# Conv layer on one core: the statistics matmuls issued one product earlier, the warm-up matmuls moved, the bias added to two images in one call

## The reference

```python
x = x + conv(group_norm(x, G=16), weight, bias)      # x: (8, 32, 128, 128) float32, weight (32, 32, 3, 3)
```

## Time and profile before

| | |
|---|---|
| median of 9 runs | 86.98 us (86.24 to 87.39) |
| the profiled execution | 86.84 us |
| its span in the profile | 85.5 us |
| busy in the span | PE 68.8, DVE 50.1, ACT 48.0, POOL 32.2 us |
| bytes moved | 33.63 MB, mean 393 GB/s over the span |

### The profile page before, as it was taken

The page is one execution under the profiler, slowest core; times in us unless marked ns, Lnnn a source line. Parts: engine busy times, 40 slices in busy tenths (PEclk is TensorE's granted clock), DMA queues, the critical chain, the costliest instruction groups (busy, mean ns, idle before and its releaser), DMA issues.

```text
span 85.5 us, 726 instructions
## 1 busy us (share of the span) xinstructions
PE 68.8 (80%) x238; PEld 42.8 (50%) x238; DVE 50.1 (59%) x43; ACT 48.0 (56%) x55; POOL 32.2 (38%) x52
## 2 busy tenths in 40 slices
PE   0011996999899989998999899989989998999300
PEld 0011453567466646674666466456746664667100
DVE  0028905971998299649946992899199815200510
ACT  6008915995796299439935992699179726000000
POOL 6729400039294005904900680076009401920000
PEclk9999999999999999999999999999999999999998
DMA  3899999999999979997998995988989488999966
GB/s 50 318 401 425 414 467 406 437 421 437 421 490 490 429 306 490 490 460 306 460 429 383 414 490 245 490 352 383 490 368 421 192 368 368 471 383 405 427 260 265
DMA packets 2209, 33.63 MB, mean 393 GB/s; under 512 B 256, under 2 KB 288, under 8 KB 416
## 3 DMA queue, kind: packets, MB, share of 16 engines
q1 hardware_dynamic: 2208, 33.62, 93.6%
HBM read 16.84 MB, written 16.78 MB: 393 GB/s over the span
## 4 chain that ended last, share of the span: by engine, by line
PE 59%; ACT 17%; DMA 8%; DVE 8%; issue 2%; SPq 1%
PE ps L380 50%; ACT g L346 12%; DMA x<-x_dram 8%; PE ps_w L413 4%; PE ps_m L308 3%; ACT std L326 3%; ACT square L315 3%; DVE rstd L332 2%; DVE var L320 2%; DVE x L395 2%; DVE rstd L329 2%; PE ps_w L253 1%; SPq L175 1%; ACT origin L283 1%
## 5 line engine op out<-in xcount | busy, mean ns | idle before, releaser
L380 PE MATMUL ps<-g,w_sb 128*128 128x363 f32 (+1 forms) x192 | 61.0, 466 | 3.1 <-ACT origin L283 2.2
L380 PEld LDWEIGHTS ps<-g,w_sb 128*128 128x128 f32 x192 | 35.1, 189 | 24.3 <-ACT origin L283 5.8
L275 DVE TENSOR_REDUCE sums<-x 128x1 f32<-128x4096 f32 (+1 forms) x9 | 35.4, 3937 | 6.2 <-DMA x<-x_dram 6.2
L364 POOL TENSOR_SCALAR x<-x,bias_sb 128x1984 f32<-128x1984 f32 (+1 forms) x16 | 24.3, 1528 | 23.1 <-ACT origin L283 18.1
L294 ACT ACTIVATE unused<-x,origin 128x4096 f32<-128x4096 f32 (+1 forms) x9 | 30.0, 3329 | 0.3
L395 DVE SCALAR_TENSOR_TENSOR x<-ps,bias_sb,x 128x1089 f32<-128x1089 f32 (+2 forms) x9 | 10.9, 1221 | 7.8 <-PE ps L380 7.8
L346 ACT ACTIVATE g<-x,rstd 128x1089 f32<-128x1089 f32 (+2 forms) x9 | 10.7, 1201 | 3.9 <-DVE rstd L332 3.9
L320 DVE TENSOR_SCALAR var<-ps_m,square 128x1 f32<-128x1 f32 x8 | 1.7, 219 | 14.1 <-ACT square L315 14.1
L315 ACT ACTIVATE square<-ps_m,origin 128x1 f32<-128x1 f32 x8 | 2.1, 261 | 12.4 <-PE ps_m L308 12.4
L247 POOL COPY pilot<-x 128x1 f32<-128x1 f32 x8 | 1.5, 185 | 18.9 <-DMA x<-x_dram 18.9
L253 PEld LDWEIGHTS ps_w<-pilot,avg 128*128 128x128 f32 x20 | 3.9, 202 | 8.3 <-POOL pilot L247 6.1
(11 more groups left out here) (17 smaller groups left out, 7.0 us busy)
## 6 DMA issues: line engine op xcount, KB each, us to landing
x<-x_dram SPq DMA_DIRECT2D x2, 4096.0 KB, 33.5
out_dram<-x SPq DMA_DIRECT2D x2, 4096.0 KB, 14.1
out_dram<-x SPq DMA_DIRECT2D x3, 2048.0 KB, 6.7
x<-x_dram SPq DMA_DIRECT2D x4, 1024.0 KB, 7.8
x<-x_dram SPq DMA_DIRECT2D x2, 2048.0 KB, 17.4
out_dram<-x SPq DMA_DIRECT2D x1, 1056.0 KB, 4.0
out_dram<-x SPq DMA_DIRECT2D x1, 992.0 KB, 8.1
wb_sb<-wb_dram SPq DMA_DIRECT2D x1, 62.0 KB, 5.0
```

The lines of the kernel that those rows point to most:

```text
L275: lambda e: e.tensor_reduce(sums[img % 2][:, k, 0:1], piece, mybir.AxisListType.X, ALU.add),
L364: put("pool", lambda e: e.tensor_scalar(part, part, 1.0, bias_sb, op0=ALU.mult, op1=ALU.add), *free, mark=True)
L380: lambda e, k=k, dc=dc, rows=rows, top=top: e.matmul(ps[:, 0:rows, 0 : N - dc], w_sb[:, k * P : (k + 1) * P], g[:, top : top + rows, dc:N] ...
```

## The change

It does six things.

1. In the loop, the group matmul of `img + 1` and the pilot of `img + 2` are issued behind seven of the first eight products, not behind all eight, and the group matmul stands ahead of the pilot.
2. `group` issues one part per call. Image 0's first half goes through the group matmul as soon as its own sums are there, its second half later.
3. The two fillers ahead of it read image 0's first rows, not those of the second half, write to a bank of `pss[1]`, not to `ps_w`, and no longer wait for `origin`.
4. The pilots of images 0 and 1 read the image itself; the copy on POOL is left for images 2 to 7. The loop's last two pilots, whose results no image uses, have no copy made for them any more.
5. `add_bias` handles images 0 and 1 in one call, then 2 and 3, and 4 to 7 singly; the pilot copies stand ahead of it in twos.
6. `avg` is made by one broadcast addition in place of an addition and three copies.

```diff
     def take_first(img, *needs):
...
-            "pool", lambda e: e.tensor_copy(pilots[img % 2], xts[img][:, 0, 0:1] if img < B else eps),
-            *(rows_in(img, 1) if img < B else ()), *needs, *([pilot_ok[img - 2]] if img > 1 else []), mark=True,
+            "pool", lambda e: e.tensor_copy(pilots[img % 2], xts[img][:, 0, 0:1]),
+            *rows_in(img, 1), *needs, *([pilot_ok[img - 2]] if img > 3 else []), mark=True,
...
     def pilot(img):
+        points = pilots[img % 2] if img > 1 else xts[img][:, 0, 0:1]
         pilot_ok[img] = put(
-            "pe", lambda e: e.matmul(ps_w[:, 0:1], avg, pilots[img % 2], start=True, stop=True),
+            "pe", lambda e: e.matmul(ps_w[:, 0:1], avg, points, start=True, stop=True),
...
-    def group(img):
+    def group(img, part=0):
         last = len(parts(img)) - 1
-        for k in range(last + 1):
...
+                ps_ms[:, 0:2], avg, sums[img % 2][:, part, :], start=(part == 0), stop=(part == last)
+            ),
+            *(sums_ok[img][part :: last + 1]), avg_ok, *means_read.get(img - 1, ()), mark=part == last,
...
-    def add_bias(img):
+    def add_bias(*imgs):
+        xt = pairs[imgs[0] // 2] if len(imgs) == 2 else xts[imgs[0]].unsqueeze(1)
+        low = xt[:, :, N:H, :].rearrange("p b h w -> p b (h w)")
+        right = xt[:, :, 0:N, N:W]
...
-                "pe", lambda e: e.matmul(ps_w, avg, piece, start=True, stop=True),
-                *rows_in(0, H), *needs, mark=True,
+                "pe", lambda e: e.matmul(pss[1][:, 0, :], avg, piece, start=True, stop=True),
+                *rows_in(0, first + FILL), *needs, mark=True,
...
-    take_first(0)
     pilot(0)
     pilot_back(0)
-    keep_warm(H // 2, 2, origin_ok[0])
     sum_up(0)
     sum_squares(0)
+    keep_warm(0, 2)
+    group(0, 0)
...
-    take_first(1, w_ok)
-    group(0)
+    group(0, 1)
     warm_ok = keep_warm(0, 1, w_ok)
     pilot(1)
     take_std(0)
     normalize(0)
-    take_first(2)
-    add_bias(0)
+    take_first(2, w_ok)
...
         multiply(img, 0)
-        multiply(img, 1)
+        multiply(img, 1, range(3))
...
+        group(img + 1)
         pilot(img + 2)
-        group(img + 1)
+        multiply(img, 1, range(3, 4))
         if img + 1 < B:
             take_std(img + 1)
             normalize(img + 1)
-            take_first(img + 3)
-            add_bias(img + 1)
+            if img < B - 4:
+                take_first(img + 3)
+            if img == B - 5:
+                take_first(img + 4)
+            if img in (0, 2):
+                add_bias(img, img + 1)
+            elif img > 2:
+                add_bias(img + 1)
         multiply(img, 2)
```

More of the change, by code:

```diff
@@ L198, in conv_preact_kernel @@
     eps = sbuf("eps", P, 1)
+    half = sbuf("half", P, 2 * C)
     avg = sbuf("avg", P, P)
@@ L215, in conv_preact_kernel @@
     pair2 = pair.rearrange("p a b -> p (a b)")
-    sums = put(
-        "pool", lambda e: e.tensor_add(avg[:, 0 : 2 * C], pair2[:, 0 : 2 * C], pair2[:, 2 * C : 4 * C]),
+    pair_ok = put(
+        "pool", lambda e: e.tensor_add(half, pair2[:, 0 : 2 * C], pair2[:, 2 * C : 4 * C]), pair_ok, mark=True
+    )
+    avg_ok = put(
+        "pool",
+        lambda e: e.tensor_add(
+            avg.rearrange("p (q c) -> p q c", q=4), *(
+                half[:, k * C : (k + 1) * C].unsqueeze(1).to_broadcast([P, 4, C]) for k in range(2)
+            )
+        ),
         pair_ok, mark=True,
     )
[L220 to L226, removed]
     put("act", lambda e: e.activation(warm, eps, AF.Sqrt), eps_ok)
@@ L246, in take_first @@
         first_ok[img] = put(
-            "pool", lambda e: e.tensor_copy(pilots[img % 2], xts[img][:, 0, 0:1] if img < B else eps),
-            *(rows_in(img, 1) if img < B else ()), *needs, *([pilot_ok[img - 2]] if img > 1 else []), mark=True,
+            "pool", lambda e: e.tensor_copy(pilots[img % 2], xts[img][:, 0, 0:1]),
+            *rows_in(img, 1), *needs, *([pilot_ok[img - 2]] if img > 3 else []), mark=True,
         )
     def pilot(img):
+        points = pilots[img % 2] if img > 1 else xts[img][:, 0, 0:1]
         pilot_ok[img] = put(
-            "pe", lambda e: e.matmul(ps_w[:, 0:1], avg, pilots[img % 2], start=True, stop=True),
-            first_ok[img], avg_ok, *([origin_ok[img - 1]] if img else []), mark=True,
+            "pe", lambda e: e.matmul(ps_w[:, 0:1], avg, points, start=True, stop=True),
+            *([first_ok[img]] if 1 < img < B else rows_in(img, 1) if img < B else []), avg_ok, *([origin_ok[img - 1]] if img else []), mark=True,
         )
@@ L300, in sum_squares @@
             )
-    def group(img):
+    def group(img, part=0):
         last = len(parts(img)) - 1
-        for k in range(last + 1):
[L306 to L310, removed]
+        ok = put(
+            "pe",
+            lambda e: e.matmul(
+                ps_ms[:, 0:2], avg, sums[img % 2][:, part, :], start=(part == 0), stop=(part == last)
+            ),
+            *(sums_ok[img][part :: last + 1]), avg_ok, *means_read.get(img - 1, ()), mark=part == last,
+        )
+        if part == last:
+            group_ok[img] = ok
     def take_std(img):
@@ L355, in normalize, with multiply @@
         normal[img].append(origin_ok[img + 1])
-    def add_bias(img):
[L359 to L365, removed]
-        ]
-    def multiply(img, n):
+    def add_bias(*imgs):
+        xt = pairs[imgs[0] // 2] if len(imgs) == 2 else xts[imgs[0]].unsqueeze(1)
+        low = xt[:, :, N:H, :].rearrange("p b h w -> p b (h w)")
+        right = xt[:, :, 0:N, N:W]
+        free = [token for img in imgs for token in (*normal[img], *sums_ok[img])]
+        free += [bias_ok] + ([warm_ok] if 0 in imgs else [])
+        marks = (len(imgs) == 2 or imgs[0] >= B - 2, True)
+        tokens = [
+            put("pool", lambda e: e.tensor_scalar(part, part, 1.0, bias_sb, op0=ALU.mult, op1=ALU.add), *free, mark=mark)
+            for part, mark in zip((low, right), marks)
+        ]
+        for img in imgs:
+            biased[img] = [token for token in tokens if token]
+    def multiply(img, n, products=range(4)):
         g = gs[img % 2]
         ps = pss[img % 2][:, n, 0 : ROWS * N].rearrange("p (r w) -> p r w", w=N)
-        for k in range(4):
+        for k in products:
             dr, dc = k // 2, k % 2
@@ L386, in multiply @@
             )
-        conv_ok[img] = [ok]
+        if ok:
+            conv_ok[img] = [ok]
     def add(img, first, last):
@@ L488, in conv_preact_kernel @@
     stored = store(to[:, 0:N, :], xt[:, 0:N, :], biased[B - 1][1], *added[B - 1])
-    put.emit_loop(NPAIR, {"act": 2 * 5, "dve": 2 * 5, "pool": 2 * 3})
+    put.emit_loop(NPAIR, {"act": 2 * 5, "dve": 2 * 5, "pool": 2 * 2})
     seen = {**put.seen["sp"]}
```

## The result

The changed kernel takes 83.64 us in the median of 10 executions (83.51 to 84.29), the kernel before 86.86 us in 31. The ratio is 0.9643 with a 95% interval of 0.9616 to 0.9670: 3.6% faster. The forecast was 83.9 us, between 83.2 and 85.2. The profiled execution took 83.66 us, and its span is 82.3 us (forecast: 82.4).

What follows compares the result with a forecast made beforehand. Transfers nearly bind: computation ends 1.4 + 2.8 = 4.2 us earlier, but closing 3.0 us of DMA gaps gives a span of 82.5, taken as 82.4; plus 1.34 is 83.74, plus 0.14 about 83.9 us, range 83.2 to 85.2.

Steps and rivals of the forecast that it cites:

- The bound: DMA stores from 43 us on: transfers nearly bind, so faster computation wins only their gaps; span 85.5 to 82.4 us.
- three gaps: Stretches near 52, 68 and 82 us where DMA engines wait for computation: about 0.7, 1.55 and 0.75, together 3.0 us.
- The start: Before image 0's products: fillers end ahead of the sums, group ends at 11.45 instead of 13.05 us, winning 1.6 us.
- Image 0: Group matmul behind seven products waits 0.45 us for image 1's squares; of the start's 1.6 us, 1.4 are left.
- the slower rival: Matmul clock low when image 0's products start; 0.5% slower if it rises later than 22.8 us; chance 0.03.
- Steady images: Loop: PE's work behind the group matmul covers the statistics, removing a wait of 0.47 us; six images make 2.8 us.
- idle time: Steady images, alternative reading: PE's wait counted as 0.31 us an image, giving 3.3 us in all with the start.
- POOL: Bias call for two images takes 3.04 to 12.2 us, should be twice 3.04, hidden behind the wait for loads.
- The computation stays the bound: Last store's data gain under 3.0 us; with the start's 1.4 us alone, 85.6 us; bound in part, chance 0.11.
- The start wins nothing, the loop all: Whole kernel: computation gains 2.8 us, span 82.7, time 84.2 us, inside the forecast's range; no separate chance.
- recover more than the gaps: DMA engines, which run apart by up to 0.5 us: span 81.65 to 81.9, time 83.2 to 83.4 us; chance 0.08.
- The term for a low clock: Image 0's products: a clock rise at 17 us costs 1.7 of the 4.2 us gain and 0.5 us of span.

Runs made afterwards that it cites:

- few stores: Changed kernel without the stores of pairs 0 and 1 and of image 6, 10 of 16 MB of results never stored: 82.38 us, ratio 0.9466.

## Why the prediction was right, point by point

**The bound.** Right: the forecast put the span at 85.5 less three gaps of 3.0 us, a little less, 82.4; it is 82.3, and the table shows that it stays there for issues of the last store down to 76.84 us. The 81.65 us that the forecast worked out for engines that end together weren't reached: they end apart (share 0.07 from 81 to 82 us).

**The start.** Group part 1 was to end at 11.45 us and the first product to start at 13.57. The timeline of the changed kernel, for the earlier trace rows:

```profile
6.03 0.56 PE L258 MATMUL ps_w<-x,avg 128*128 128x1 f32 x2 [6.03 <-DMA x<-x_dram]
...
6.44 3.76 PE L427 MATMUL ps<-x,avg 128*128 128x512 f32 x4
...
10.71 0.19 ACT L299 ACTIVATION_READ_ACCUMULATOR unused<-x,origin 128x1 f32 x1
...
10.96 0.38 PE L312 MATMUL ps_m<-sums,avg 128*128 128x2 f32 x2 [0.54 <-ACT unused L299]
...
11.20 1.10 PE L427 MATMUL ps<-x,avg 128*128 128x512 f32 x2
...
13.47 6.18 PE L393 MATMUL ps<-g,w_sb 128*128 128x363 f32 x14 [1.05 <-ACT g L354]
...
18.05 0.19 ACT L299 ACTIVATION_READ_ACCUMULATOR unused<-x,origin 128x1 f32 x1
...
23.47 5.54 POOL L375 TENSOR_SCALAR x<-x,bias_sb 128x3968 f32<-128x3968 f32 x2
```

The fillers end ahead of the sums, the group part takes 0.38 us (between the bounds of 0.33 and 0.59), and the product starts at 13.47. Right.

**Image 0.** Wrong in its cause, and the size off: the wait for the squares (0.45 us) never came, since they ended at 18.24 while PE was still at its seven products, which ended at 19.65. The clock was low and they took 6.18 us instead of 4.44. The group matmul ended at 19.77, not 18.7, and image 1's products were to win 1.4 us and won about 0.5: they started at 22.83 instead of 23.31, without waiting for `g`. Image 1's first piece, before and after:

```profile
23.31 0.57 PE L380 MATMUL ps<-g,w_sb 128*128 128x363 f32 x1 [0.31 <-ACT origin L283]
```

```profile
22.83 0.47 PE L393 MATMUL ps<-g,w_sb 128*128 128x363 f32 x1
```

The low clock is the slower rival's mechanism, which was given a small chance as a whole and a price for a part: "A rise at 17 us costs 1.7 us of 4.2, and 0.5 us of the span". The clock was full again by 17.4 us and the 14 pieces cost 1.74 us more. With the clock up, in the run with one filler more, the wait did come, with 0.40 us, and from the first product to the end of the group matmul it took 5.27 us where the forecast had 5.13: the term was right for a clock that stays up. The span lost nothing by the low clock, because of the next point.

**Steady images.** The term was mis-sized: 0.47 us an image was forecast, by the starts of the pieces, and the period fell by 0.58, from 8.13 to 7.55. The first piece behind the pause had also taken 0.57 us, where without a pause it takes 0.47 (the two lines above), which the idle time and the last start don't show. Six images by 0.58 are 3.5 us. With the 0.5 us of image 0 that makes 4.0; forecast 4.2, measured 4.08 at the last store. Two errors of about 0.8 us cancelled: the total was right by luck, and the changed kernel's second profile has 4.67 us. Of the two readings that the forecast set side by side, idle time (0.31) is off by almost a factor of two; the Trainium skill's warning about matmul busy time, in "Trainium Kernel Development and Optimization", section Performance Expectations, holds here, and even the starts gave too little.

**POOL.** Right: a call for two images took 5.54 us against 6.1 forecast, from 23.47 to 29.0, and nothing waited for it.

**Rivals.** "The computation stays the bound" is what the run without the loop's order shows, at 86.88 instead of the 85.6 that was worked out. In its profiled execution the start gained 1.52 us, the slow pieces took back 0.77, and 0.78 were left at the last store; of its slower executions there is no profile. That PE's wait would move to the loop's branch didn't happen: the group matmuls follow each other evenly. "The start wins nothing, the loop all" is nearly what happened: the loop's order alone takes 83.70, where 84.2 was worked out from the smaller term. The DMA engines didn't recover more than the gaps in the forecast's sense: 82.3 is the shortest profiled span of the kernels that store everything.

**Where it was lucky.** The forecast held a low clock to be unlikely because PE has work "without a pause over 1 us". The pause ahead of the first product was 1.05 us, in a stretch in which PE was busy for 0.43 of 1.4 us, and the clock fell. The term for a low clock, put at a small chance, cost 1.74 us of the computation, and only the transfers hid it. Without the loop's part the same start was worth nothing that can be told from zero.

## What to carry to other kernels

Before adding up what each part of a change saves, find the second bound and its distance: here about 3 us of empty transfer time, read from windows with a share near zero, was what the computation could win, and anything more was wasted. Place the one issue that ends the program (the last store) against the time when its engine comes free: on one side of that time the span follows it one for one, on the other not at all. Matmuls moved forward for warming leave a pause behind them; look at what PE does just ahead of the first product, not at how much warming there is, and judge the clock by the time of a piece beside the clock row.

## What was not expected of the hardware

In the changed kernel's profile the granted clock fell to 0.50 at about 13.9 us, just as the products began, though PE had run two group parts, one filler and a pilot behind the first fillers. It was full again by 17.4 us, in the profile of few stores by 20.2. The page "TensorE: Matmul & The Clock Gate" of the Trainium skill, Part 1, says that the point of change varies from run to run; these two profiles agree.

The clock row doesn't show every low stretch. In the changed kernel the first four filler pieces take 0.94 us each, where the two later ones take 0.55 each (1.10 us for both), and the row reads 1.00 for all of them. The second profile of the kernel with single bias calls shows what that can hide (PE's timeline, and a window as above):

```profile
11.42 2.05 PE L427 MATMUL ps<-x,avg 128*128 128x512 f32 x2
...
13.70 5.59 PE L393 MATMUL ps<-g,w_sb 128*128 128x363 f32 x14
```

```profile
14.00:17.00 3.00, 3.00 (x7) 1.00 1.02 437
```

PE starts 7 pieces in these 3 us, as many as in the changed kernel, whose row reads 0.50 there. Nine profiles have the new start and one filler behind the group matmul. In four of them the filler's two pieces take 1.10 us, then the clock falls ahead of the products or just as they begin, and the first seven products take 6.04 to 7.49 us. In the other five the two pieces take 2.05 or 2.06 us and no fall is recorded, but the first seven take 5.32 to 6.65 us (without the loop's order, the first eight 5.85), against 4.48 with the clock up. So what the low clock costs differs from execution to execution, between 0.8 and 3.0 us. The mean granted clock doesn't tell it: it is 0.991 in the profile above, and lies between 0.951 and 0.989 in the changed kernel's first executions, at spans of 82.2 to 82.5.

The kernel with single bias calls has about 0.5 us more outside the span, in two groups of runs, and nothing more inside it. Its profiles show a load of instructions behind the span; that this is the cause isn't shown.
